# Negative-part sums moved behind the last units' passes, the score weights' products into the first norm's wait, and turned gates read later, in a graph and mixture-of-experts kernel

## The reference

```python
x = x + where(adj < 1, exp(-(1/adj - 1)**2 / 0.5), 0) @ (z @ W + B)       # layer 0 graph
x = x + sum over the top 2 of 8 experts: gate * (relu(z @ W1 + b1) @ W2 + b2)  # layer 0 experts
x = x + de * gru_edge(adj0 @ z, z) + dn * gru_node(mean of 3 heads, z)    # layer 1 graph
x = x + sum over the top 2 of 8 experts: gate * ((silu(z @ w1) * (z @ w3)) @ w2)  # layer 1 experts
```

## Time and profile before

| | |
|---|---|
| median of 3 runs | 554.35 us (553.42 to 555.64) |
| profiled execution | 556.78 us, span 554.0 us |
| TensorE busy | 484.3 us, 87% of the span |
| its weight loads | 298.2 us, 54% |
| VectorE busy | 389.2 us, 70% |
| ScalarE busy | 268.6 us, 48% |
| GpSimd busy | 117.2 us, 21% |
| chain that ended last | TensorE 53%, VectorE 26%, ScalarE 10%, issue 8% |
| mean granted clock of TensorE | 0.941 of full speed |

### The profile page before, as it was taken

One profiled execution on the slowest core, in us unless ns is written; L12 is line 12 of the kernel. 1 busy time (PEld: TensorE's weight loads), 2 busy tenths in 40 slices (PEclk: granted clock), 3 DMA queues, 4 the chain that ended last, 5 costly groups with the idle time before them and its releaser, 6 DMA issues.

```text
span 554.0 us, 6085 instructions
## 1 busy us (share of the span) xinstructions
PE 484.3 (87%) x1850; PEld 298.2 (54%) x1850; DVE 389.2 (70%) x709; ACT 268.6 (48%) x443; POOL 117.2 (21%) x171
## 2 busy tenths in 40 slices
PE   5474879888789989989799999899898998998996
PEld 3322534444456645546344444335466776776896
DVE  1998989766576822257648959767868967778674
ACT  5988797668676421042431232202324456565553
POOL 3000000000010000000000001886204454546564
PEclk9677689979799999899999999979998999999999
DMA  8870000000000010000000000432032221312350
GB/s 286 293 215 4 0 0 0 1 1 0 1 1 1 2 50 1 0 1 1 1 0 1 9 20 1 102 92 59 3 94 56 64 70 56 98 58 49 64 91 16
DMA packets 23640, 25.79 MB, mean 47 GB/s; under 512 B 2565, under 2 KB 18960, under 8 KB 23604
## 3 DMA queue, kind: packets, MB, share of 16 engines
q1 hardware_dynamic: 23604, 25.36, 16.8%
HBM read 24.61 MB, written 0.74 MB: 46 GB/s over the span
## 4 chain that ended last, share of the span: by engine, by line
PE 53%; DVE 26%; ACT 10%; issue 8%; POOL 1%; DVEq 0%; POOLq 0%; ACTq 0%
PE bank L1284 10%; PE bank L942 6%; PE bank L944 6%; PE bank L943 5%; PE bank L1114 4%; PE bank L1232 3%; DVE pr_ring L1879 3%; PE bank L971 3%; PE bank L1075 2%; PE bank L1273 2%; DVE y_units L1425 2%; DVE y_units L1436 2%; DVE hr_ring L1695 2%; DVE t_units L1431 2%; DVE y_units L1446 1%
## 5 line engine op out<-in xcount | busy, mean ns | idle before, releaser
L1284 PE MATMUL bank<-pr_ring,hW 128*128 128x512 f32 (+3 forms) x198 | 95.1, 566 | 6.1 <-DVE pr_ring L1879 5.4
L1879 DVE SCALAR_TENSOR_TENSOR pr_ring<-adjT,regR,bank 128x512 f32<-128x512 f32 (+3 forms) x99 | 64.7, 679 | 30.5 <-PE bank L1273 28.9
L1892 DVE TENSOR_TENSOR adjT<-bank,adjT 128x512 f32<-128x512 f32 (+1 forms) x66 | 41.3, 626 | 29.2 <-ACT bank L891 28.9
L1284 PEld LDWEIGHTS bank<-pr_ring,hW 128*128 128x128 f32 (+1 forms) x198 | 35.0, 194 | 36.5 <-DVE pr_ring L1879 18.5
L942 PE MATMUL bank<-z3hi,w13hi 128*128 128x512 f32 (+4 forms) x132 | 50.7, 384 | 3.6 <-DVE adjT L1892 3.6
L971 PE MATMUL bank<-y_units,msg 128*128 128x512 f32 (+3 forms) x66 | 36.2, 689 | 18.2 <-DVE y_units L1446 18.2
L891 ACT ACTIVATE bank<-bank 128x512 f32<-128x512 f32 (+1 forms) x66 | 35.0, 531 | 34.9 <-PE bank L944 34.8
L944 PE MATMUL bank<-z3hi,w13lo 128*128 128x512 f32 (+4 forms) x132 | 49.0, 371 | 0.0
L943 PE MATMUL bank<-z3lo,w13hi 128*128 128x512 f32 (+4 forms) x132 | 48.7, 369 | 0.0
L603 POOL TENSOR_TENSOR prr_ring<-adjT,adjTr 128x512 fp32r<-128x512 f32 (+4 forms) x34 | 36.4, 1069 | 56.5 <-ACT adjTr L880 52.1
L1075 PE MATMUL bank<-hr_ring,W2s 128*128 128x512 f32 (+1 forms) x96 | 46.5, 572 | 0.0
(11 more groups left out here) (268 smaller groups left out, 1014.8 us busy)
## 6 DMA issues: line engine op xcount, KB each, us to landing
adjT<-rows SPq DMA_DIRECT2D x16, 256.0 KB, 3.4
stage<-in_w SPq DMA_DIRECT2D x8, 341.0 KB, 3.0
adjT<-in_adjT SPq DMA_DIRECT2D x1, 2560.0 KB
adjT<-in_adjT SPq DMA_DIRECT2D x1, 1650.0 KB
adjT<-in_adjT SPq DMA_DIRECT2D x3, 512.0 KB, 6.0
adjT<-rows SPq DMA_DIRECT2D x8, 165.0 KB, 4.2
adjT<-in_adjT SPq DMA_DIRECT2D x1, 1024.0 KB
W1f<-in_W SPq DMA_DIRECT2D x1, 1024.0 KB, 12.0
```

The costliest lines, as they stand in the source:

```text
L1284: nc.tensor.matmul(B_ACC[:, 0:w], hW[0:r, j, k * P:(k + 1) * P], ring[0:r, 0:w], start=(k == 0 and j == 0), stop=(k == K - 1 and j == T - ...
L1879: nc.vector.scalar_tensor_tensor(out=pr_ring[0:r, 4 + p % R_RING, 0:w], in0=adjT[0:r, j, cols(c)], scalar=g_col[0:r, j, k:k + 1], in1=B_F[ ...
L1892: nc.vector.tensor_tensor(halves(sg, w), halves(B_H1[h_bank(q)][0:r, 0:w], w), gate_buf(n)[0:r, :, :], ALU.mult).then_inc(s["s_gated"], 1)
```

## The change

Three groups of entries move in the tables, and `v` leaves the tables. The work is the same.

- `v` goes on TensorE from behind turn(0) at step 1 to between `var` and `logits` of the first norm, and on VectorE from step 2 to between cutoff(6) and route(0).
- The sums stood at steps 14, 20, 21, 23 (two), 25, 26, 27, 28, 31 and 33, and stand now at 23, 24, 25, 26, 27, 29, 30, 32, 34, 35 and 37.
- turn(3) is read by VectorE at (6, 9) and not at (6, 7). turn(5) is made by TensorE behind tile 38 and not 36, and read by VectorE behind tile 39 and not 37.

```diff
--- before.py
+++ after.py
@@ -93,24 +93,24 @@
 
 
 PE0 = {
-    1: [("turn", 0), ("v",)], 3: [("unit", 6)], 4: [("unit", 7)], 6: [("unit", 8)], 7: [("unit", 9)], 11: [("unit", 10), ("unit", 11)],
-    12: [("mean", 1, 1)], 13: [("var", 1, 1)], 15: [("logits", 1)], 17: [("turn", 1)], 18: [("unit", 12)], 19: [("mean", 2, 0)],
-    20: [("var", 2, 0), ("unit", 13)], 22: [("unit", 14)], 23: [("unit", 15)], 24: [("unit", 16), ("unit", 17)], 26: [("mean", 1, 2)],
-    28: [("var", 1, 2)], 30: [("logits", 2)], 32: [("htok", 0)], 33: [("turn", 2), ("hw", 0)], 34: [("hw", 1)], 35: [("hw", 2)], 36: [("hw", 3)],
-    37: [("mean", 2, 1)], 38: [("var", 2, 1)], 41: [("htok", 1)], 42: [("hw", 4)], 43: [("hw", 5)], 45: [("hw", 6)], 46: [("hw", 7)]}
+    1: [("turn", 0)], 3: [("unit", 6)], 4: [("unit", 7)], 6: [("unit", 8)], 7: [("unit", 9)], 11: [("unit", 10), ("unit", 11)], 12: [("mean", 1, 1)],
+    13: [("var", 1, 1)], 15: [("logits", 1)], 17: [("turn", 1)], 18: [("unit", 12)], 19: [("mean", 2, 0)], 20: [("var", 2, 0), ("unit", 13)],
+    22: [("unit", 14)], 23: [("unit", 15)], 24: [("unit", 16), ("unit", 17)], 26: [("mean", 1, 2)], 28: [("var", 1, 2)], 30: [("logits", 2)],
+    32: [("htok", 0)], 33: [("turn", 2), ("hw", 0)], 34: [("hw", 1)], 35: [("hw", 2)], 36: [("hw", 3)], 37: [("mean", 2, 1)], 38: [("var", 2, 1)],
+    41: [("htok", 1)], 42: [("hw", 4)], 43: [("hw", 5)], 45: [("hw", 6)], 46: [("hw", 7)]}
 ACT0 = {
     0: [("sq", 9), ("ln", 9), ("arg", 7), ("exp", 7), ("inv", 9)], 2: [("arg", 8), ("sq", 10), ("ln", 10), ("inv", 10)], 3: [("exp", 8)],
     4: [("arg", 9), ("exp", 9)], 5: [("sq", 11), ("ln", 11), ("inv", 11)], 6: [("sq", 12), ("arg", 10), ("ln", 12), ("exp", 10), ("inv", 12)],
-    7: [("arg", 11)], 8: [("exp", 11), ("sq", 13), ("ln", 13), ("inv", 13)], 12: [("center", 1, 1)], 13: [("var", 1, 1)], 14: [("neg", 0)],
+    7: [("arg", 11)], 8: [("exp", 11), ("sq", 13), ("ln", 13), ("inv", 13)], 12: [("center", 1, 1)], 13: [("var", 1, 1)],
     15: [("rank", 1), ("sq", 14), ("ln", 14), ("inv", 14)], 16: [("sq", 15), ("ln", 15), ("inv", 15)], 17: [("arg", 12), ("exp", 12)],
     18: [("sq", 16), ("arg", 13), ("ln", 16), ("exp", 13), ("inv", 16)],
-    19: [("center", 2, 0), ("sq", 17), ("arg", 14), ("ln", 17), ("exp", 14), ("inv", 17)], 20: [("arg", 15), ("exp", 15), ("neg", 1)],
-    21: [("var", 2, 0), ("arg", 16), ("exp", 16), ("neg", 2)], 22: [("arg", 17), ("exp", 17)], 23: [("neg", 3), ("neg", 4)], 25: [("neg", 5)],
-    26: [("neg", 6)], 27: [("center", 1, 2), ("neg", 7)], 28: [("var", 1, 2), ("neg", 8)], 31: [("rank", 2), ("neg", 9)], 32: [("htok", 0)],
-    33: [("hw", 0), ("neg", 10)], 34: [("hw", 1)], 35: [("hw", 2)], 36: [("hw", 3)], 37: [("center", 2, 1)], 38: [("var", 2, 1)], 39: [("htok", 1)],
-    41: [("hw", 4)], 43: [("hw", 5)], 45: [("hw", 6)], 46: [("hw", 7)]}
+    19: [("center", 2, 0), ("sq", 17), ("arg", 14), ("ln", 17), ("exp", 14), ("inv", 17)], 20: [("arg", 15), ("exp", 15)],
+    21: [("var", 2, 0), ("arg", 16), ("exp", 16)], 22: [("arg", 17), ("exp", 17)], 23: [("neg", 0)], 24: [("neg", 1)], 25: [("neg", 2)],
+    26: [("neg", 3)], 27: [("center", 1, 2), ("neg", 4)], 28: [("var", 1, 2)], 29: [("neg", 5)], 30: [("neg", 6)], 31: [("rank", 2)],
+    32: [("htok", 0), ("neg", 7)], 33: [("hw", 0)], 34: [("hw", 1), ("neg", 8)], 35: [("hw", 2), ("neg", 9)], 36: [("hw", 3)],
+    37: [("center", 2, 1), ("neg", 10)], 38: [("var", 2, 1)], 39: [("htok", 1)], 41: [("hw", 4)], 43: [("hw", 5)], 45: [("hw", 6)], 46: [("hw", 7)]}
 DVE0 = {
-    0: [("sign", 8), ("cut", 7), ("mult", 8)], 1: [("step", 8), ("sign", 9)], 2: [("v",), ("mult", 9)], 3: [("step", 9), ("cut", 8)],
+    0: [("sign", 8), ("cut", 7), ("mult", 8)], 1: [("step", 8), ("sign", 9)], 2: [("mult", 9)], 3: [("step", 9), ("cut", 8)],
     4: [("sign", 10), ("mult", 10), ("step", 10)], 5: [("cut", 9)], 6: [("sign", 11), ("mult", 11), ("step", 11)], 7: [("cut", 10)],
     8: [("sign", 12), ("mult", 12)], 9: [("cut", 11), ("step", 12)], 10: [("sign", 13), ("mult", 13)],
     11: [("x1", 1), ("center", 1, 1), ("step", 13)], 13: [("scale", 1, 1)], 15: [("rank", 1), ("sign", 14), ("turn", 1)],
@@ -140,8 +140,8 @@
     (1, 7): [("top", 1)], (2, 0): [("share", 1)], (2, 1): [("rest", 1, 0)], (2, 2): [("rest", 1, 1)], (2, 4): [("mid", 0, 2)],
     (2, 6): [("blend", 0, 2)], (2, 7): [("add", 0, 2)], (2, 10): [("top", 2)], (3, 3): [("share", 2)], (3, 4): [("rest", 2, 0)],
     (3, 8): [("mid", 1, 0)], (3, 10): [("rest", 2, 1)], (4, 1): [("blend", 1, 0)], (4, 4): [("add", 1, 0)], (4, 8): [("center", 3, 0)],
-    (5, 0): [("scale", 3, 0)], (5, 7): [("scores", 3)], (6, 4): [("shares", 3), ("ranks", 3)], (6, 6): [("weights", 3)], (6, 7): [("turn", 3)],
-    (6, 9): [("mid", 1, 1)], (7, 2): [("blend", 1, 1)], (7, 4): [("add", 1, 1)], (7, 6): [("center", 3, 1)], (8, 5): [("scale", 3, 1)],
+    (5, 0): [("scale", 3, 0)], (5, 7): [("scores", 3)], (6, 4): [("shares", 3), ("ranks", 3)], (6, 6): [("weights", 3)],
+    (6, 9): [("turn", 3), ("mid", 1, 1)], (7, 2): [("blend", 1, 1)], (7, 4): [("add", 1, 1)], (7, 6): [("center", 3, 1)], (8, 5): [("scale", 3, 1)],
     (8, 7): [("scores", 4)], (8, 10): [("shares", 4)]}
 MAIN_ACT = [
     ("spread", 3), ("spread", 4), ("spread", 5), ("turned", 1), ("spread", 6), ("spread", 7), ("gates", 0, 1), ("spread", 8), ("new", 0, 1),
@@ -149,13 +149,13 @@
     ("factor", 2), ("support", 0), ("gates", 1, 0), ("part", 2, 0), ("turned", 5), ("part", 2, 1), ("new", 1, 0), ("part", 2, 2), ("table",),
     ("turned", 6), ("turned", 7), ("turned", 8), ("center", 3, 0), ("var", 3, 0), ("rank", 3), ("support", 1), ("table", "tanh"), ("gates", 1, 1),
     ("new", 1, 1), ("center", 3, 1), ("table",), ("var", 3, 1), ("rank", 4)]
-PE1 = {0: [("gates", 1, 2)], 1: [("mid", 1, 2)], 9: [("turn", C + 1)], 12: [("mean", 3, 2)], 16: [("var", 3, 2)],
-       28: [("logits", C + 2)], 36: [("turn", C + 2)]}
+PE1 = {
+    0: [("gates", 1, 2)], 1: [("mid", 1, 2)], 9: [("turn", 4)], 12: [("mean", 3, 2)], 16: [("var", 3, 2)], 28: [("logits", 5)], 38: [("turn", 5)]}
 ACT1 = {0: [("gates", 1, 2)], 1: [("new", 1, 2)], 14: [("center", 3, 2)], 17: [("table",), ("var", 3, 2)],
         30: [("table",), ("rank", C + 2)]}
-DVE1 = {0: [("mid", 1, 2)], 1: [("blend", 1, 2)], 2: [("add", 1, 2)], 5: [("ranks", C + 1)], 7: [("weights", C + 1)],
-        9: [("turn", C + 1)], 13: [("center", 3, 2)], 18: [("scale", 3, 2)], 29: [("scores", C + 2)], 31: [("shares", C + 2)],
-        32: [("ranks", C + 2)], 34: [("weights", C + 2)], 37: [("turn", C + 2)]}
+DVE1 = {
+    0: [("mid", 1, 2)], 1: [("blend", 1, 2)], 2: [("add", 1, 2)], 5: [("ranks", 4)], 7: [("weights", 4)], 9: [("turn", 4)], 13: [("center", 3, 2)],
+    18: [("scale", 3, 2)], 29: [("scores", 5)], 31: [("shares", 5)], 32: [("ranks", 5)], 34: [("weights", 5)], 39: [("turn", 5)]}
 GBUF = 5
 SPLIT_AFTER = 4 * T + 5
 THREE = 6
@@ -1057,6 +1057,7 @@
                 sums(g)
             side(("mean", 1, 0))
             side(("var", 1, 0))
+            side(("v",))
             pe.wait_ge(s["ffn0_in"], 80)
             side(("logits", 0))
             at(pe, "W1_lo", 2)
```

## The result

The changed kernel takes **556.66 us** (median of 17 runs, 552.22 to 557.55); 17 runs of the kernel before beside them give 554.51. The ratio is **1.0029, 95% interval 1.0015 to 1.0043**: 1.6 us slower where the prediction had 1.85 us faster, and 556.66 is outside its range of 549.7 to 555.3.

What follows compares the result with a forecast made beforehand. TensorE was taken as busy for most of the span but handed work late by VectorE and ScalarE in the first half. Terms +2.1 - 2.6 + 0.45 - 0.2 - 1.6 = -1.85 us took 554.35 to 552.5, range 549.7 to 555.3.

Steps and rivals of the forecast that it cites:

- v, +2.1: First norm: products v start only when TensorE's wait ends, and logits then wait for the wcat copy; 2.1 us slower.
- Rival (b): First norm: the products' delay is absorbed, or they run inside the wait; -3.95 us, 550.4; chance 0.15.
- Sums 1 and 2, -2.6: Ahead of relu(21) and relu(22): sums leave ScalarE's queue, so the unit products come 2.6 us earlier; bounds 0 and -2.9.
- the late sums, +0.45: Steps 32 to 37: four sums for one on ScalarE delay the norm's logarithm; 0.45 us slower, bounds 0 and +4.0.
- Rival (c): Steps 33 to 38: ScalarE becomes the pace, sums cost 4.0 and not 0.45; 556.05 us; chance 0.12.
- The clock, "so I take 0": Behind the wait ending at 141 us: the shorter wait leaves the low clock unchanged; 0, ends -1.7 and +1.7.
- The bound of 1.7: Clock at 144 to 148 us: about 3.4 us at half speed cost some 1.7 us, taken as -1.7 and +1.7.
- Turn 3, -0.2 with bounds 0 and -1.8: First range: two more numerators precede VectorE's read of the transposes, which it had waited 1.78 us for; 0.2 us faster.
- Turn 5, -1.6: Third range: TensorE's 1.99 us wait at the transposes goes, 0.4 is lost again at tile 37; 1.6 us faster.
- Rival (d): Third range: gates come late and VectorE waits at tile 44; +0.75 us, 555.1; chance 0.08.

Runs made afterwards that it cites:

- the broadcasts: Changed kernel with step 24's gate broadcast put ahead of units 16 and 17 and done four times: 553.96 us, ratio 0.9985 to the kernel before.

## Why the prediction was wrong

- **v, +2.1: right.** 2.1 to 2.2 in each profile, by the instructions named. The ratios say 0.4%, 2.1 to 2.4 us. Rival (b) is out. The 1.0 us that most profiles give back before 121 us was not foreseen, and the ratios don't show it.
- **Sums 1 and 2, -2.6: right as a stretch** (-2.62), and **the late sums, +0.45: right** (+0.38). Rival (c) is out. One count was wrong: at steps 23 to 30 six sums had stood, not eight, so ScalarE has one more there and not one less. Yet by the ratios all the sums together gain about nothing (below), where the text had 2.15 us.
- **The clock, "so I take 0": the second step that failed.** At 140 to 148 us itself 0 was nearly right, profile against profile: the clock is as low as before, and 137 to 149 us takes 0.3 more. The rule that the text weighed against this (the Trainium skill, TensorE: Matmul & The Clock Gate, section "HAM oscillation — how this bites in real kernels", that only long idle gaps need be avoided) doesn't hold here: a wait of 1.87 us was followed by a granted clock of 0.64 and 0.51. But the one profile of before was no measure of the kernel before, and what counts is how much useful work falls into the low stretch. In 137 to 149 us the eleven sums-moved kernels without broadcasts average 11.72 us, the six others without broadcasts 10.96. In 178 to 243 us, a place the text did not look at, eight of those eleven have 65.4 and five of the six others 63.8. Together +0.8 and +0.9 on average, against -2.6 + 0.4. The bound of 1.7 was too small as well: it counted the low stretch from 144 us only, and with the broadcasts and a clock of 1.00, 137 to 149 us alone takes 2.5 less. The edit that removed this fall pays in the changed kernel; that the clock is all of the missing gain is not, since the ratios with and without the sums differ by +0.04% alone, +0.21% in the changed kernel and -0.35% beside turn 5, each uncertain by about 0.3%.
- **Turn 3, -0.2 with bounds 0 and -1.8: the step that made it wrong.** Its local effect was right: VectorE comes some 0.4 us earlier. But half a microsecond puts two waits that were harmless where the clock falls, 1.2 us in 404 to 410 and 1.2 in 410 to 430. The text followed the numerators and the gates and priced nothing for the clock here; no rival had a gain that turns into a loss 20 us later. By the ratios turn 3 costs 0.3% (1.7 us) with turn 5 moved and 0.6% without.
- **Turn 5, -1.6: right mechanism, a little large.** -1.4, with the 0.4 lost again at tile 37 measured as 0.54. Rival (d) is out: the gates came in time. With turn 3 late it is worth 0.37% by the ratios, as it also takes away a wait behind which a fall came in both profiles that have it beside a late turn 3.
- **The sum.** With the measured terms (+2.2, -2.6 + 0.4, +1.7 for the clock, +2.0 for turn 3, -1.4) it is +2.3 us where 1.6 was measured (2.15 between the medians): the sign comes from the two clock terms, and the one of +1.7 is an average over kernels, not shown part by part. The frame was read rightly: one profiled execution is not a median.

## What to carry over

In a kernel near TensorE's pace, cost an edit also by what it does to the waits behind it: the same two waits of 0.55 us were free or cost 2.4 us, by half a microsecond of position. Compare the granted clock stretch by stretch in several profiles with and without the edit, and before giving up a gain try to fill the wait with harmless repeated work, and measure it: filling 0.9 of the 4.49 us wait in the kernel before cost 0.43%. One part of a bundled change can carry its loss: try each part alone and left out.

## What was not expected of the hardware

In seven profiles two waits of only 0.57 and 0.54 us, 1.03 us apart, were followed by a fall of TensorE's clock to its lower level (1.2 GHz); in eight with the same two waits it stayed at 1.00. TensorE was busy 2.89 of the 4 us in either case (404 to 408 us, changed kernel and kernel before). The distance from the fall near 357 us to the end of the second wait separates the two groups: 47.79 and 47.93 us are the nearest two with and without a fall. At the units, waits of 3.57 and 1.87 us were followed by a fall, and waits of 0.93 and 0.97 in one profile and not in another. Repeated products that compute nothing made the changed kernel 0.7% faster.
